# A transformer block on one core: the routing stage with three input buffers, scaling a block ahead, and the shift on VectorE

## The reference

```python
h = layernorm(x) * (1 + ca) + sa
x = x + ga * (causal_attention(h) @ Wc)     # 16 heads of 16 channels
h = layernorm(x) * (1 + cb) + sb
logits = h @ gate_w.T + expert_bias         # 8 experts and 4 pass-through ones
two best of 12 per token, softmax over the two -> w
x = x + gb * (sum over chosen experts of w * expert(h) + w_zero * h)
```

## Time and profile before

| | us |
|---|---|
| median of 3 runs (2793.20 to 2794.93) | 2794.07 |
| the profiled execution, its own time | 2799.72 |
| its span | 2798.0 |
| `route` in it, from 2004 to 2203.3 | 199.3 |

### The profile page before, as it was taken

One profiled execution on the slowest core, in us unless ns is written; L12 is line 12 of the kernel. 1 busy time (PEld: TensorE's weight loads), 2 busy tenths in 40 slices (PEclk: granted clock), 3 DMA queues, 4 the chain that ended last, 5 costly groups with the idle time before them and its releaser, 6 DMA issues. The chain is left out here.

```text
span 2798.0 us, 46776 instructions
## 1 busy us (share of the span) xinstructions
PE 2536.4 (91%) x16092; PEld 1312.3 (47%) x16093; DVE 1906.6 (68%) x3194; ACT 1671.1 (60%) x2989; POOL 745.2 (27%) x692
## 2 busy tenths in 40 slices
PE   6985899999999999999999999999676579879898
PEld 4553233333333333333333333332265479779788
DVE  5985888878878878878888888781066556445433
ACT  2655037777777777777777777778532245435444
POOL 2544300111011011011011011011046747636533
PEclk8998579999999999999999999999887689989999
DMA  5798901541550451452353244000286666546434
GB/s 168 215 250 221 148 16 36 103 73 56 104 100 20 90 101 29 81 101 38 72 101 48 62 77 62 17 17 14 79 237 188 177 149 127 96 82 114 82 63 63
DMA packets 214886, 271.22 MB, mean 97 GB/s; under 512 B 27280, under 2 KB 176304, under 8 KB 212272
## 3 DMA queue, kind: packets, MB, share of 16 engines
q1 hardware_dynamic: 175408, 221.01, 35.8%
q0 software_dynamic: 32160, 41.57, 8.7%
q10 hardware_dynamic: 7136, 6.32, 0.7%
HBM read 136.30 MB, written 131.74 MB: 96 GB/s over the span
## 5 line engine op out<-in xcount | busy, mean ns | idle before, releaser
L1073 DVE TENSOR_REDUCE mxc<-ps 128x2 f32<-128x1024 f32 (+4 forms) x1168 | 1297.8, 1148 | 294.9 <-PE ps L981 182.6
L1054 ACT ACTIVATE probs<-ps 128x512 f32<-128x512 f32 (+1 forms) x2240 | 1184.3, 588 | 401.7 <-PE ps L1011 371.9
L1011 PE MATMUL ps<-qs,ks 99*128 99x512 bf16 (+3 forms) x2560 | 736.5, 350 | 6.5 <-ACT probs L1054 4.5
L981 PE MATMUL ps<-ks,qs 96*128 96x512 bf16 (+3 forms) x2560 | 696.7, 362 | 48.4 <-PEq L262 35.3
L1027 PE MATMUL ps<-probs,vs 128*32 128x512 f32 (+3 forms) x5120 | 600.0, 541 | 1.2 <-issue 0.5
L1011 PEld LDWEIGHTS ps<-qs,ks 99*128 99x128 bf16 x2560 | 216.1, 97 | 606.7 <-ACT probs L1054 461.2
L939 POOL TENSOR_SCALAR_AFFINE_SELECT probs<-probs 128x512 f32<-128x512 f32 x256 | 162.2, 634 | 993.3 <-ACT probs L1054 993.3
L981 PEld LDWEIGHTS ps<-ks,qs 96*128 96x128 bf16 x2560 | 240.7, 99 | 262.2 <-DVE mxc L1073 61.8
L1665 PE MATMUL ps<-x_t,w_at 128*128 128x128 f32 x2000 | 253.1, 281 | 9.3 <-ACT x_t L1696 8.4
L1665 PEld LDWEIGHTS ps<-x_t,w_at 128*128 128x128 f32 x2000 | 248.6, 197 | 22.1 <-issue 14.0
L1766 POOL DMA_INDIRECT out<-ys,idx x122 | 194.1, 1591 | 227.9 <-DMA out<-ys,idx 109.4
(11 more groups left out here) (172 smaller groups left out, 1830.2 us busy)
## 6 DMA issues: line engine op xcount, KB each, us to landing
ks<-k_parts SPq DMA_DIRECT2D x96, 256.0 KB, 13.0
qs<-q_parts SPq DMA_DIRECT2D x96, 256.0 KB, 14.6
xs<-slot_x SPq DMA_DIRECT2D x128, 131.0 KB, 2.1
v_ones<-vout SPq DMA_DIRECT2D x64, 256.0 KB, 3.5
vs<-v_ones SPq DMA_DIRECT2D x16, 1024.0 KB, 26.2
attn_t<-o_sb SPq DMA_DIRECT2D x64, 256.0 KB, 3.1
slot_x<-zero SPq DMA_DIRECT2D x24, 655.0 KB, 9.6
q_parts<-parts SPq DMA_DIRECT2D x96, 128.0 KB, 2.5
```

Of the source, the lines that this page charges most:

```text
L981: ins = pe.matmul(o[:, h, :], qs[r][0:SROWS, h0 + h, i * P:(i + 1) * P], ks[r][0:SROWS, h0 + h, 512 * c:512 * c + w], start=first, stop=no ...
L1011: ins = pe.matmul(o[:, h, :], ks[r][0:SROWS + MROWS, h0 + h, j * P:(j + 1) * P], qs[r][0:SROWS + MROWS, h0 + h, J * QJ + lo:(J + 1) * QJ], ...
L1054: act.activation(probs[:, (NKT * r + m) % NPB, h0:h0 + nh, 0:QJ - lo], st_view(r, s), ACT.Exp, scale=DH ** -0.5).then_inc(exp_done, 1)
L1073: dve.tensor_reduce(mxc[:, h0:h0 + nh, i, c], red_view(u, at), AX_X, ALU.max).then_inc(red_done, 1)
```

## The change

`num` and `rbc` get three buffers instead of two, and `load(t)` waits for the output matmuls of block t-3 instead of t-2. `h2s` gets two buffers, and POOL's multiply of block t waits for the shift of block t-2. The shift (adding sb) leaves POOL and becomes a stage `shift` of DVE. On DVE the turn becomes attended(s), positions(s-7), shift(s-4), residual(s-2), top2(s-5), scales(s-2), chosen(s-5). The turns of PE, ACT, POOL and SP stay as they are.

```diff
-        XB = 4
-        num, rbc = sb("num", [P, 2, KC, BLK]), sb("rbc", [P, 2, KC, BLK])
+        XB, AB = 4, 3
+        num, rbc = sb("num", [P, AB, KC, BLK]), sb("rbc", [P, AB, KC, BLK])
-        hn, h2s, h2_t = sb("hn", [P, TPB, C]), sb("h2s", [P, TPB, C]), sb("h2_t", [P, TPB, KC, P])
+        hn, h2s, h2_t = sb("hn", [P, TPB, C]), sb("h2s", [P, 2, TPB, C]), sb("h2_t", [P, TPB, KC, P])
...
                 def load(t):
-                    b, par, tok = t // BPS, t % 2, t % BPS * BLK
-                    if t >= 2:
-                        sp.wait_ge(out_done, t - 1)
+                    b, par, tok = t // BPS, t % AB, t % BPS * BLK
+                    if t >= AB:
+                        sp.wait_ge(out_done, t - AB + 1)
...
                 def attended(t):
-                    par = t % 2
-                    dve.wait_ge(o_ld[par], 16 * 2 * KC * (t // 2 + 1))
+                    par = t % AB
+                    dve.wait_ge(o_ld[par], 16 * 2 * KC * (t // AB + 1))
...
+                def shift(t):
+                    b = t // BPS
+                    dve.wait_ge(mult_done, t + 1)
+                    dve.tensor_tensor(r["h2"][:, TPB * t:TPB * (t + 1), 0:C], h2s[:, t % 2, :, :],
+                                      wide(k["sbc"][:, b, 0, None, :], 1, TPB), ALU.add).then_inc(mod_done, 1)
+
...
-                blocks((0, attended), (1, residual), (3, top2), (1, scales), (4, chosen), (6, positions))
+                blocks((0, attended), (7, positions), (4, shift), (2, residual), (5, top2), (2, scales), (5, chosen))
...
                 def modulate(t):
                     b = t // BPS
                     pool.wait_ge(hn_done, t + 1)
-                    if t >= 1:
-                        pool.wait_ge(mod_done, t)
+                    if t >= 2:
+                        pool.wait_ge(mod_done, t - 1)
                     apart(pool)
-                    pool.tensor_tensor(h2s[:, :, :], hn[:, :, :], wide(k["sbc"][:, b, 1, None, :], 1, TPB), ALU.mult).then_inc(mult_done, 1)
-                    pool.wait_ge(mult_done, t + 1)
-                    apart(pool)
-                    pool.tensor_tensor(r["h2"][:, TPB * t:TPB * (t + 1), 0:C], h2s[:, :, :], wide(k["sbc"][:, b, 0, None, :], 1, TPB),
-                                       ALU.add).then_inc(mod_done, 1)
+                    pool.tensor_tensor(h2s[:, t % 2, :, :], hn[:, :, :], wide(k["sbc"][:, b, 1, None, :], 1, TPB),
+                                       ALU.mult).then_inc(mult_done, 1)
```

More of the change, by code:

```diff
@@ L1251, in route @@
         std, rstd, nmr = sb("std2", [P, TPB]), sb("rstd2", [P, TPB]), sb("nmr2", [P, TPB])
-        hn, h2s, h2_t = sb("hn", [P, TPB, C]), sb("h2s", [P, TPB, C]), sb("h2_t", [P, TPB, KC, P])
+        hn, h2s, h2_t = sb("hn", [P, TPB, C]), sb("h2s", [P, 2, TPB, C]), sb("h2_t", [P, TPB, KC, P])
         lg = sb("lg", [P, TPB, ET])
-        o_ld = [sem(f"o{j}") for j in range(2)]
+        o_ld = [sem(f"o{j}") for j in range(AB)]
         x_ld = [sem(f"x{j}") for j in range(XB)]
@@ L1310, in output @@
                         for c in range(KC):
-                            ins = pe.matmul(pc[t % 2][:, n, :], num[:, t % 2, c, n * P:(n + 1) * P], k["wc"][:, t // BPS, c, :],
+                            ins = pe.matmul(pc[t % 2][:, n, :], num[:, t % AB, c, n * P:(n + 1) * P], k["wc"][:, t // BPS, c, :],
                                             start=(c == 0), stop=(c == KC - 1))
```

## The result

The changed kernel takes 2828.08 us (median of 4 runs, 2822.28 to 2829.30) against 2794.02: a ratio of 1.0118 (95% interval 1.0100 to 1.0135), 34.1 us slower. The forecast was 2824.8.

What follows compares the result with a forecast made beforehand. No engine is full; a 9.92 us ring of waits between PE and DVE bounds `route`. 26.9 us to attended(15) plus 3.8 at the end is 30.7: 2799.72 becomes 2830.4, median 2824.8 us, range 2805 to 2840.

Steps and rivals of the forecast that it cites:

- PE no longer waits for DVE: Steady part of `route`: output finds numerators scaled a block earlier, top2 uses earlier logits; the 9.92 us ring is gone.
- The new ring: SP's queue: load(s+1) waits behind store(s-2), which waits for residual after attended and shift; period 12.3 us instead of 9.92.
- VectorE's part: DVE's share of the new ring per block, attended, shift and residual's add: 1.14 + 1.14 + 1.24 = 3.52 us.
- The latency: From the end of residual's add through store and load to the next attended: 8.8 us per block, thirteen loads.
- Positions: DVE's positions stage, between attended(12) and shift(8): stays on the ring in full, 13.4 us.
- The start: First blocks of `route`: load(2) no longer waits for output(0), so attended(2) comes 5.9 us earlier.
- POOL's multiply: Ends 8.05 us after residual's add, before attended at 8.8; nearly a floor, since an earlier attended would run into it.
- The end: After attended(15): 43.7 us with PE at low clock, 35.7 at high; middle 39.7, 3.8 more than before.
- The range: Latency 7.9 to 9.4 and the end -4 to +4 give 2811 to 2836 us; widened to 2805 to 2840.
- Rival 1: Loads run a block ahead in `route`, period 8.3 us, kernel 2774.8 us; chance 0.06.
- Rivals 2 and 3: Rival 2: POOL's multiply slides under attended, up to 2.07 us per block, 2852 us, likelier 2838; chance 0.08.
- rival 3: No difference: a load alone moves faster, 3.0 instead of 5.5 us, latency 6.3, kernel 2792 us; chance 0.04.

Runs made afterwards that it cites:

- e1: Changed kernel with store lag 3 instead of 2, so load(s+1) is queued ahead of store(s-2) on SP: 2783.3 us, 0.9965 of the kernel before.
- e4: Changed kernel without the rbc loads from block 3 on, reciprocals of blocks 0 to 2 reused: 2807.6 us, 1.0054 of the kernel before.
- e3: Changed kernel with the shift back on POOL, behind its multiply: 2830.5 us, 1.0129 of the kernel before.
- e5: e1 with PE's turn reordered, output ahead of normed: 2776.8 us, 0.9937 of the kernel before.
- e6: e1 with four buffers of num and rbc instead of three: 2769.9 us, 0.9914 of the kernel before.

## Why the prediction was right

The range, the sign and the mechanism held; that the number came so near is in part luck, since errors of two terms cancel. By its own steps:

- *PE no longer waits for DVE*: shown for the ring of the earlier trace rows, where `output` waited for `attended` and `top2` for the logits; both waits are gone in the steady part. Taken word for word the heading is wrong: the transposes now wait 4.4 us for the shift on DVE, which costs nothing in this ring and stands in the ring of e1.
- *The new ring* through SP's queue: shown by e1, which moves one entry of that queue and takes 44.8 us away, and by e4, where the time follows the size of the load.
- *VectorE's part*, 3.52: measured 3.53 (2080.83 to 2084.36).
- *The latency*, 8.8: the term that was mis-sized. From the store's issue to attended it was 8.23 to 10.87 us, 9.24 in the mean of thirteen, so 13 x 0.44 = 5.7 us were missing. Most of that came in the last three blocks, where POOL's scatters are under way as well: they took 10.1 in the mean, the first ten 9.0. e3 has 9.9 and 8.8, e4 with its half loads 7.8 and 6.5, so it is there each time; the forecast has no term for it, and that the scatters are the reason was not tried. The 9.38 of the earlier trace rows, left whole, would have been nearer only by luck, since these loads have no tables in front.
- *Positions*, 13.4 in full: 2144.35 to 2157.76, 13.41.
- *The start*: attended(2) 10.6 us after attended(0), forecast 10.8.
- *POOL's multiply* 8.05 us after residual's add: 2076.55 + 2.35 - 2070.96 = 7.94, and the exclusion did not strike: attended lasts 1.22 us in all sixteen blocks. That it would strike an earlier load, so that 8 us were nearly a floor, is shown by e4, and e3 shows the same with POOL's add. The Trainium skill (SBUF — State Buffer, Who interferes with whom) calls the shared pair of ports an exclusive lock and says that the order of issue decides who blocks. The 2.89 and 3.15 us agree with the lock. They do not agree with a wait for the whole of POOL's instruction and the full 1.22 us behind it, since attended ends 1.08 us after POOL; and in one case of the 28 (e1, attended at 2143.54, 3.96 us) attended had begun 0.51 us before the multiply and still ended behind it.
- *The end*: forecast 39.7 us from attended(15), 3.8 more than before; measured 36.4 (2197.57 to 2234.0), 0.6 more. The 39.7 was the middle between 43.7 with PE at the low clock (its terms add up to 43.6) and 35.7, for which no working was given. PE did not stay at the low clock:

```profile
2209.55 3.62 PE L1311 MATMUL ps<-wc,num 128*128 128x256 f32 x16
```

  against the 6.29 of the earlier trace rows. This error of -3.2 and the latency's of +5.7 leave 2.5, the distance from the forecast 30.7 to the 33.1 us by which `route` grew.
- *The range*: latency and end added up give 2809 to 2837, not 2811 to 2836; the stated 2805 to 2840 holds both.

Rival 1 had a sound thought, that three buffers can hide the loads; it needed SP's order changed too, and e1 shows it with 2783.3 against the 2774.8 that the rival gave. Rivals 2 and 3 did not occur: the multiply stayed clear, and the load kept nearly its length. Of its 512 packets of 2 KB, 479 moved from 2087 to 2091 in the changed kernel (4 us, 251 GB/s); in the kernel before it was 488 from 2073 to 2078 (5 us, 203 GB/s). Both are slower than the 3.0 us of rival 3, although next to nothing else was under way.

## What to carry to other kernels

Before an instruction is moved a turn later on one engine, look for every queue in which something unrelated stands behind a wait for it: here a store of finished rows, waiting a block longer, held back the next load, and a third buffer could not help since the queue never reached it. A lag has to be changed on all engines together; one number in SP's order turned a loss of 1.2% into a gain of 0.35%, and with a fourth buffer of 0.86%. When engines all become emptier after a change, look for a transfer whose latency stands in a ring.

## What the runs showed of the hardware

`attended`, a VectorE instruction with two inputs in SBUF, is not slowed in proportion when it meets POOL's multiply or add. In e1, e3, e4, e5 and e6 it ended 1.07 to 1.10 us after POOL's, however early it began: 28 times, with durations from 1.41 to 3.96 us instead of 1.22. The other way round, where attended had begun first, it kept its 1.23 us and POOL's instruction ended 2.19 to 2.22 us after it, 13 times over all ten kernels, with durations from 2.74 to 3.34 us instead of 2.35. One case fits neither: the 3.96 us of e1, where attended began before the multiply and was blocked all the same. Residual's add, whose one input lies in PSUM, overlapped POOL's multiply or add 53 times and took 1.21 to 1.23 us each time.

One load of 512 packets of 2 KB (1.05 MB) took 4 to 5 us with next to nothing else under way, 203 to 251 GB/s, while in e6, with four buffers and several loads queued, the same DMA engines moved 308 GB/s in the mean over 50 us. So such a load by itself does not reach what they can carry. Why is not shown: it may be the number of packets in flight, but the 1 KB packets of the earlier trace rows reached 349 GB/s without several loads queued, so the kind of transfer may matter as much. No run varied either alone, and the 308 hold x_in and the stores too.
